# A postponed first transpose, a reordered normalisation and block transposes over every fourth key, in an attention kernel on one core

## The chip, the core and the metric

The kernel runs on one core of a Trainium2 chip. The time is that of the device for the whole program, in microseconds (us), as the median of several executions. The core has a matrix engine (TensorE, PE in the profile; its weight loads are PEld), a vector engine (VectorE, DVE), an activation engine (ScalarE, ACT), a general engine (GpSimd, POOL) and a queue for transfers (SyncE, SP). Each runs its own list of instructions in order and waits for the others on semaphores.

## The reference

The input x has 8 sequences of 1024 tokens with 256 channels. Attention with 16 heads of 64, then a residual sum and a layer norm; behind it a mixture of eight experts with a second residual sum and layer norm. The change touches only attention:

```python
latent_kv = x @ w_kv_down                # rank 128
k, v = split(latent_kv @ w_kv_up)        # 16 heads of 64
q = x @ w_q
att = einsum('bqhd,bkhd->bhqk', q, k) * 64 ** -0.5
att = softmax(where(causal, att, -inf), axis=-1)
y = einsum('bhqk,bkhd->bqhd', att, v)
x = layernorm(x + y @ w_out)
```

## The kernel before

attention_stage handles two heads (a pair) at a time, 64 pairs in all (8 sequences of 8 pairs). For each pair n it goes through eight tiles q of 128 queries. A "slot" is one step (n, q); each engine has a function `slot(n, q)` that lists by hand what it issues there. Causality makes tile q see q + 1 tiles of keys, so the tiles grow from 128 to 1024 columns. Score s = 2q + h is that of tile q for head h.

For a score: TensorE computes it (line 330), VectorE adds the mask and takes the maximum (`maximum`, line 651), ScalarE computes the exponential into one of eight buffers `prob` and the row sum (`exp`, line 514), VectorE inverts the sum (`invert`, line 657), and GpSimd multiplies the row by it (`norm`, line 209). The probabilities must then be turned, so that keys lie along the partitions, before they are multiplied with v (`pv`, line 376). There are two ways:

- tiles 0 to 3: TensorE transposes them (`turn`, line 358), ScalarE copies them out of PSUM into `tri` (`copy_turned`, line 532), one copy is VectorE's (line 672).
- tiles 4 to 7: VectorE transposes blocks of 32 by 32 (`turn_squares`, line 665) into `squares`. Four such blocks side by side are the keys of one tile of keys. SP writes `squares` to DRAM (`write_squares`, line 262) and reads it back with four transfers of 32 partitions each (`read_squares`, line 272) into `late_t`. In the kernel before, block j holds keys 32j to 32j + 31 and lands in partitions 32j to 32j + 31.

The same slots also hold the projections of q, k and v (lines 413 to 415, 426 to 428, 441) for the next pair, which are computed in a single PSUM bank, so that each waits for ScalarE's copy of the one before (`keep`, line 520, and `copy_v`, line 525). They use the weights split in a high part (ScalarE, line 546) and a low part (`weights_low`, GpSimd, line 215).

The counters set the order. `norm_done` counts normalised scores, so whoever waits for one must know its place in GpSimd's list. `exp` of scores 0 to 7 of a pair reuses buffers that hold scores 8 to 15 of the pair before, and waits until VectorE has turned them (`squared`). Scores share three areas of PSUM: those of tile 4 wait for the exponentials of tiles 2 and 3 (`scores_free`).

Behind the last pair, TensorE waits for the last reads of `late_t`, and then the output stage and the expert stage follow.

Of the kernel before, what the change touches and what calls it, by code (L numbers as in the profile page):

```python
# [17 lines left out]
P = 128  # L18
# [4 lines left out]
NPAIR = NH // 2  # L23
# [41 lines left out]
def attention_stage(nc, x_t, w_down, w_q, w_k, w_v, y_d, s_d, w_out, R):  # L65
# [4 lines left out]
    with ExitStack() as ctx:  # L70
# [95 lines left out]
        def y_place(n, g):  # L166
            return min(2 * n + 3, 2 * NPAIRS) if g else max(2 * n, 1)

        def last_of_batch(n):
            return n % NPAIR == NPAIR - 1 and n < NPAIRS - 1  # L170

# [18 lines left out]
        @block.gpsimd  # L190
        def _(pool):
            for free in (*pv_done, y_copied, *y_out):
                pool.sem_inc(free, 1)
            pool.memset(ident[:], 0.0).then_inc(const_ready, 1)
            pool.wait_ge(const_ready, 1)
            pool.affine_select(out=ident[:], in_=ident[:], compare_op=ALU.not_equal, fill=1.0, base=0,
                               pattern=[[-1, P]], channel_multiplier=1).then_inc(const_ready, 1)
            pool.wait_ge(const_ready, 2)
            pool.memset(mask[:], 0.0).then_inc(const_ready, 1)
            pool.wait_ge(const_ready, 3)  # L200
            pool.affine_select(out=mask[:, T - P:T], in_=mask[:, T - P:T], compare_op=ALU.is_ge, fill=-MASKED, base=0,
                               pattern=[[-1, P]], channel_multiplier=1).then_inc(const_ready, 1)

            def norm(n, q):
                pool.wait_ge(inv_done, 8 * n + q + 1)
                pool.sem_inc(passed, 1)
                for i in (2 * q % PB, 2 * q % PB + 1):
                    pr = prob[i][:, 0:(q + 1) * P]
                    pool.tensor_scalar(pr, pr, inv[:, i:i + 1], 1.0, ALU.mult, ALU.mult).then_inc(norm_done, 1)  # L209

            def weights_low(n):
                u = n % 2
                pool.wait_ge(w_high, n + 1)
                pool.sem_inc(passed, 1)
                pool.tensor_tensor(wqk_lo[u][:], wqk[u][:], wqk_hi[u][:].bitcast(F32), ALU.subtract).then_inc(w_low, 1)

            def x_low_part(b, i):
                k, cols = x_piece(i)
                pool.wait_ge(x_high, 4 * b + i + 1)
                pool.sem_inc(passed, 1)  # L220
                pool.tensor_tensor(xt_lo[:, k, cols], xt[:, k, cols], xt_hi[:, k, cols].bitcast(F32), ALU.subtract
                                   ).then_inc(x_low, 1)

            def l_low_part(b, i):
                pool.wait_ge(l_step, 4 * b + 2 * i + 2)
                pool.sem_inc(passed, 1)
                pool.tensor_tensor(lat_lo[:, halves(i)], lat[:, halves(i)], lat_hi[:, halves(i)].bitcast(F32),
                                   ALU.subtract).then_inc(l_low, 1)

            weights_low(0)  # L230

            def slot(n, q):
                norm(n, q)
                for i in x_pieces(n, q):
                    x_low_part(n // NPAIR + 1, i)
                if q == 0 and n + 1 < NPAIRS:
                    weights_low(n + 1)
                if last_of_batch(n) and q in (2, 3):
                    l_low_part(n // NPAIR + 1, q - 2)

            over_pairs(slot)

        @block.sync
        def _(sp):
# [19 lines left out]
            def read_squares(n, q):  # L264
                t = q + 1
                sp.wait_ge(squares_out[q % 2], 16 * (2 * n + (q - 4) // 2 + 1))
                sp.sem_inc(passed, 1)
                if q == 4 and n >= 2:
                    sp.wait_ge(pv_done[1], n)
                    sp.sem_inc(passed, 1)  # L270
                for j in range(4):
                    sp.dma_start(late_t[n % 2][Q * j:Q * j + Q, q - 4, :, 0:2 * t * Q],
                                 s_d[q - 4, :, 2 * j * t * Q:2 * (j + 1) * t * Q].rearrange("(i p) c -> p i c", p=Q)
                                 ).then_inc(late_in[n % 2], 16)

# [46 lines left out]
        def _(pe):  # L322
# [26 lines left out]
            def turn(n, q):  # L349
                if q:  # L350
                    pe.wait_ge(copied, 4 * n + q)
                elif n:
                    pe.wait_ge(exp_done, 16 * n)
                for h in range(2):
                    pe.wait_ge(norm_done, 16 * n + 2 * q + h + 1)
                    for j in range(q + 1):
                        to = q - j if h else j
                        mm = pe.transpose(turned_part(n, q, h)[:, to * P:(to + 1) * P],  # L358
                                          prob[(2 * q + h) % PB][:, j * P:(j + 1) * P], ident[:])
                    mm.then_inc(turned, 1)  # L360
# [92 lines left out]
            def slot(n, q):  # L453
# [9 lines left out]
                if q == 1:  # L463
                    if n >= 2:
                        pv(n - 2, 1, [6, 7])
                    project_v(n, 0)
                    turn(n, 0)
                if q == 2:
                    project_v(n, 1)
                    turn(n, 1)  # L470
                if q == 3:
                    if last_of_batch(n):
                        project_l(n // NPAIR + 1, 0)
                        turn(n, 2)
                        project_q(n + 1, 0)
                    else:
                        if after:
                            project_q(n + 1, 0)
                        turn(n, 2)
                if q == 4:  # L480
                    if last_of_batch(n):
                        project_l(n // NPAIR + 1, 1)
                        turn(n, 3)
                        project_k(n + 1, 0)
                    else:
                        if after:
                            project_k(n + 1, 0)
                        turn(n, 3)
                    if after:
                        project_k(n + 1, 1)  # L490
                if q == 5:
                    if after:
                        project_q(n + 1, 1)
                    pv(n, 0, range(4))
                if q == 6 and n:
                    pv(n - 1, 1, [0, 1, 2])
# [8 lines left out]
        def _(act):  # L505
# [74 lines left out]
            def slot(n, q):  # L580
# [15 lines left out]
                if q == 2:  # L596
                    if n >= 2:
                        copy_y(n - 2, 1)
                    copy_turned(n, 0)
                    exp(n, 4)  # L600
                    copy_v(n, 1)
                    exp(n, 5)
                if q == 3:
                    copy_turned(n, 1)
                    exp(n, 6)
                    if new:
                        l_split(n // NPAIR + 1, 0)
                    exp(n, 7)
                if q == 4:
                    if new:  # L610
                        copy_turned(n, 2)
                    if after:
                        keep(n + 1, 0)
                    if new:
                        l_split(n // NPAIR + 1, 1)
                    else:
                        copy_turned(n, 2)
                        if after:
                            keep(n + 1, 1)
                    exp(n, 8)  # L620
                    copy_turned(n, 3, [0])
                    if new:
                        keep(n + 1, 1)
                    exp(n, 9)
                if q == 5:
                    if after:
                        keep(n + 1, 2)
                    exp(n, 10)
                    if after:
                        keep(n + 1, 3)  # L630
                    exp(n, 11)
                if q == 6:
                    copy_y(n, 0)
# [11 lines left out]
        def _(dve):  # L645
# [10 lines left out]
                dve.wait_ge(exp_done, 16 * n + 2 * q + 2)  # L656
                dve.reciprocal(inv[:, i:i + 2], total[:, i:i + 2]).then_inc(inv_done, 1)  # L657

            def turn_squares(n, q):
                t = q + 1  # L660
                for h in range(2):
                    dve.wait_ge(norm_done, 16 * n + 2 * q + h + 1)
                    if h == 0:
                        dve.wait_ge(squares_out[q % 2], 16 * (2 * n + (q - 4) // 2))
                    dve.transpose(square_all(q).rearrange("p (j h k c) -> p j h k c", j=4, h=2, c=Q)[:, :, h, :, :],  # L665
                                  prob[(2 * q + h) % PB][:, 0:t * P].rearrange("p (k j c) -> p j k c", j=4, c=Q)
                                  ).then_inc(squared, 1)

            def copy_turned_last(n):
# [20 lines left out]
                                  ALU.subtract).then_inc(l_low, 1)  # L690

            def slot(n, q):
                maximum(n, 2 * q)
                if q == 3:
                    invert(n, 2)
                if q == 5:
                    invert(n, 4)
                maximum(n, 2 * q + 1)
                if q == 0 and n:
                    turn_squares(n - 1, 6)  # L700
                if q == 1:
                    if n:
                        invert(n - 1, 7)
                    invert(n, 0)
                if q == 2:
                    invert(n, 1)
                    if n:
# [2 lines left out]
                    invert(n, 3)  # L710
                if q == 4:
                    copy_turned_last(n)
                if q == 6:
                    invert(n, 5)
                    turn_squares(n, 4)
                if q == 7:
                    invert(n, 6)
                    turn_squares(n, 5)
                if n == NPAIRS - 1 and q < 4:
                    wo_low(q)  # L720

# [1288 lines left out]
```

## Time and profile before

| | us |
|---|---|
| median of 3 runs | 3476.64 |
| lowest and highest run | 3470.68, 3477.32 |
| the profiled execution | 3472.87 |
| its span of instructions | 3471.0 |
| TensorE busy in the span | 2987.7 |
| VectorE, ScalarE, GpSimd busy | 1971.3, 1776.9, 1568.1 |

The profile is one execution. Its page gives the busy time of each engine and cuts the span into 40 equal slices of 86.8 us; the attention stage fills slices 1 to 28. Groups name the line, the engine and what is written and read. A timeline lists instructions of one engine in order, those of one line and form merged; the number in brackets is how long the engine was idle before and who released it.

### The profile page before, as it was taken

How to read it: one execution, taken by the hardware profiler on the slowest of the kernel's cores; microseconds unless marked ns; L12 is line 12 of the kernel's file. 1: busy time of each engine (PE TensorE's matmuls, PEld its weight loads, DVE VectorE, ACT ScalarE, POOL GpSimd, SP SyncE). 2: the span in 40 equal slices, each digit the busy share in tenths (PEclk: the TensorE clock that was granted, in tenths of full speed). 3: DMA queues.
4: the chain of work that ended last, by engine and by line, in shares of the span. 5: the costliest groups of instructions: out<-in, count | busy, mean ns of one | idle time of the engine just before them, and what ended most of it. 6: DMA issues, size and time to landing. Idle time of an engine off the chain costs nothing. (4 is left out here: it accounts for less than half of the span.)

```text
span 3471.0 us, 53404 instructions
## 1 busy us (share of the span) xinstructions
PE 2987.7 (86%) x17196; PEld 1986.9 (57%) x17196; DVE 1971.3 (57%) x4808; ACT 1776.9 (51%) x3981; POOL 1568.1 (45%) x1661
## 2 busy tenths in 40 slices
PE   7788888887888887888888888885998999999997
PEld 4444444443444444444444444443998999999997
DVE  4555555555555555555555555554397885455446
ACT  5555555555555555555555555553544444444443
POOL 2334334333333433433343333331676777666665
PEclk9899899899898999899999998997999999999998
DMA  4886886887778777877877868878774444444335
GB/s 119 215 226 187 220 225 189 221 215 207 207 205 223 204 202 223 214 196 210 230 187 214 229 184 225 217 193 242 268 258 139 119 100 106 104 106 101 78 73 150
DMA packets 345525, 644.62 MB, mean 186 GB/s; under 512 B 36360, under 2 KB 244616, under 8 KB 337056
## 3 DMA queue, kind: packets, MB, share of 16 engines
q1 hardware_dynamic: 303200, 590.68, 61.4%
q0 software_dynamic: 25152, 33.75, 5.8%
q10 hardware_dynamic: 16896, 16.78, 1.4%
q8 instruction: 139, 2.28, 0.3%
q14 instruction: 138, 1.13, 0.1%
HBM read 347.38 MB, written 293.69 MB: 185 GB/s over the span
## 5 line engine op out<-in xcount | busy, mean ns | idle before, releaser
L209 POOL TENSOR_SCALAR prob<-prob,inv 128x128 f32<-128x128 f32 (+7 forms) x1024 | 748.9, 745 | 1485.0 <-DVE inv L657 1485.0
L651 DVE CUSTOM_DVE_ANT_0 s_ps<-s_ps,mask 128x128 f32<-128x128 f32 (+7 forms) x1024 | 756.6, 771 | 985.1 <-PE s_ps L330 985.1
L514 ACT ACTIVATE prob<-s_ps,neg_max 128x128 f32<-128x128 f32 (+7 forms) x1024 | 755.3, 739 | 820.3 <-DVE neg_max L651 820.3
L358 PE MATMUL s_ps<-ident,prob 128*128 128x128 f32 x1280 | 237.8, 313 | 357.6 <-POOL prob L209 357.6
L665 DVE STREAM_TRANSPOSE squares<-prob 128x640 f32<-128x640 f32 (+3 forms) x512 | 500.1, 1015 | 2.1 <-DMA s_d<-squares 2.1
L376 PE MATMUL o_ps<-late_t,v 128*64 128x512 f32 (+3 forms) x2048 | 414.5, 526 | 46.2 <-DMA late_t<-s_d 45.5
L358 PEld LDWEIGHTS s_ps<-ident,prob 128*128 128x128 f32 x1280 | 155.6, 152 | 445.9 <-issue 408.8
L330 PE MATMUL s_ps<-tok 64*128 64x512 f32 (+3 forms) x1536 | 344.9, 556 | 10.3 <-ACT tri L532 7.3
L330 PE MATMUL s_ps<-k,q 64*128 64x512 f32 (+3 forms) x1536 | 344.1, 554 | 10.6 <-ACT tri L532 7.8
L1670 PE MATMUL e_y<-w_hi,hid_hi 128*128 128x256 f32 (+1 forms) x1088 | 312.1, 287 | 0.0
L1672 PE MATMUL e_y<-w_hi,hid_lo 128*128 128x256 f32 (+1 forms) x1088 | 308.2, 283 | 0.0
L1671 PE MATMUL e_y<-w_lo,hid_hi 128*128 128x256 f32 (+1 forms) x1088 | 308.2, 283 | 0.0
L1531 POOL DMA_INDIRECT acc_d<-yg,idx_all x128 | 211.0, 1648 | 189.8 <-ACT yg L1744 155.8
L376 PEld LDWEIGHTS o_ps<-late_t,v 128*64 128x64 f32 x2048 | 124.9, 136 | 281.8 <-issue 187.1
L1778 ACT ACTIVATE raw<-e_h,b1s 128x384 f32<-128x384 f32 (+3 forms) x336 | 193.8, 586 | 133.9 <-PE e_h L1653 128.2
L330 PEld LDWEIGHTS s_ps<-tok 64*128 64x128 f32 x1536 | 135.7, 199 | 181.3 <-issue 128.1
L330 PEld LDWEIGHTS s_ps<-k,q 64*128 64x128 f32 x1536 | 134.8, 198 | 180.4 <-issue 120.3
L1651 PE MATMUL e_h<-tok_hi,w_hi 128*128 128x384 f32 (+3 forms) x672 | 229.9, 342 | 1.7 <-DVE tok_lo L1816 1.2
L1652 PE MATMUL e_h<-tok_lo,w_hi 128*128 128x384 f32 (+3 forms) x672 | 229.8, 342 | 0.0
L1653 PE MATMUL e_h<-tok_hi,w_lo 128*128 128x384 f32 (+3 forms) x672 | 229.4, 341 | 0.0
L532 ACT ACTIVATE tri<-s_ps 128x128 f32<-128x128 f32 (+3 forms) x448 | 164.4, 412 | 119.3 <-PE s_ps L358 114.0
L441 PEld LDWEIGHTS j_ps<-wv,b_lat 128*128 128x128 f32 x1024 | 173.9, 257 | 80.0 <-issue 79.4
(233 smaller groups left out, 5545.1 us busy)
## 6 DMA issues: line engine op xcount, KB each, us to landing
s_d<-squares SPq DMA_DIRECT2D x64, 1024.0 KB, 5.1
late_t<-s_d SPq DMA_DIRECT2D x256, 256.0 KB, 6.9
s_d<-squares SPq DMA_DIRECT2D x64, 896.0 KB, 7.0
late_t<-s_d SPq DMA_DIRECT2D x256, 224.0 KB, 6.6
s_d<-squares SPq DMA_DIRECT2D x64, 768.0 KB, 4.0
late_t<-s_d SPq DMA_DIRECT2D x256, 192.0 KB, 6.9
s_d<-squares SPq DMA_DIRECT2D x64, 640.0 KB, 2.9
late_t<-s_d SPq DMA_DIRECT2D x256, 160.0 KB, 5.1
```

Source lines behind the costliest of these rows:

```text
L209: pool.tensor_scalar(pr, pr, inv[:, i:i + 1], 1.0, ALU.mult, ALU.mult).then_inc(norm_done, 1)
L330: mm = pe.matmul(score_part(n, 2 * q + h)[:, w], q_of[n % 2][rows, cols], k_of[n % 2][rows, w], start=True, stop=True)
L358: mm = pe.transpose(turned_part(n, q, h)[:, to * P:(to + 1) * P], prob[(2 * q + h) % PB][:, j * P:(j + 1) * P], ident[:])
L376: mm = pe.matmul(o_ps[64 * h:64 * h + 64, off:HALF], v[n % 2][:, k, 64 * h:64 * h + 64], keys, start=(k == 0), stop=(k == 4 * g + 3), skip ...
L514: act.activation(prob[i][:, 0:(q + 1) * P], score_part(n, s), ACT.Exp, scale=-1.0, bias=neg_max[:, i:i + 1], accum_out=total[:, i:i + 1]). ...
L651: dve.tensor_tensor_reduce(part, part, mask[:, T - (q + 1) * P:T], 1.0, -MASKED, ALU.add, ALU.min, neg_max[:, i:i + 1]).then_inc(max_done, 1)
L665: dve.transpose(square_all(q).rearrange("p (j h k c) -> p j h k c", j=4, h=2, c=Q)[:, :, h, :, :], prob[(2 * q + h) % PB][:, 0:t * P].rear ...
L1651: pe.matmul(out, w1_hi[u][:, w], tok_hi[:, k, 0:N], start=(k == 0), stop=False)
L1652: pe.matmul(out, w1_hi[u][:, w], tok_lo[:, k, 0:N], start=False, stop=False)
L1670: pe.matmul(out, hid_hi[:, m, cols], w2_hi[u][:, w], start=(m == 0), stop=False)
L1671: pe.matmul(out, hid_hi[:, m, cols], w2_lo[u][:, w], start=False, stop=False)
L1672: mm = pe.matmul(out, hid_lo[:, m, cols], w2_hi[u][:, w], start=False, stop=(m == HC - 1))
```

## The change

TensorE issues its transposes of tiles 0, 1 and 2 one slot later, those of tile 3 stay in slot 4; the last projection of q moves from slot 5 to slot 4, ahead of the scores of tile 5. ScalarE's copies follow. GpSimd normalises tile 7 of a pair behind tile 0 of the next, and splits the next weights one slot later, behind tile 1. VectorE turns tile 4 in slot 5 rather than 6, tile 5 at the head of slot 7, and tile 6 in slot 1 of the next pair, one head ahead of the inverse of tile 0 and one behind it. The block transposes read every fourth column of a tile, so that block j holds keys j, j + 4, j + 8 and so on, and the read back into `late_t` puts it into partitions j, j + 4, j + 8. What `late_t` holds in the end is the same.

```diff
+        def normal(n, q, h):
+            place = {0: max(8 * n - 1, 0), 7: min(8 * n + 8, 8 * NPAIRS - 1)}.get(q, 8 * n + q)
+            return 2 * place + h + 1
@@ GpSimd
             def slot(n, q):
-                norm(n, q)
+                if q < 7:
+                    norm(n, q)
+                if q == 0 and n:
+                    norm(n - 1, 7)
+                if q == 1 and n + 1 < NPAIRS:
+                    weights_low(n + 1)
                 for i in x_pieces(n, q):
                     x_low_part(n // NPAIR + 1, i)
-                if q == 0 and n + 1 < NPAIRS:
-                    weights_low(n + 1)
@@ SP
-                    sp.dma_start(late_t[n % 2][Q * j:Q * j + Q, q - 4, :, 0:2 * t * Q],
+                    sp.dma_start(late_t[n % 2][j:P:4, q - 4, :, 0:2 * t * Q],
@@ TensorE
                 if q == 1:
...
                     project_v(n, 0)
-                    turn(n, 0)
                 if q == 2:
                     project_v(n, 1)
-                    turn(n, 1)
+                    turn(n, 0)
                 if q == 3:
...
                         if after:
                             project_q(n + 1, 0)
-                        turn(n, 2)
+                        turn(n, 1)
                 if q == 4:
...
                         if after:
                             project_k(n + 1, 0)
-                        turn(n, 3)
+                        turn(n, 2)
                     if after:
                         project_k(n + 1, 1)
-                if q == 5:
+                    turn(n, 3)
                     if after:
                         project_q(n + 1, 1)
+                if q == 5:
                     pv(n, 0, range(4))
@@ ScalarE
                 if q == 2:
                     if n >= 2:
                         copy_y(n - 2, 1)
-                    copy_turned(n, 0)
                     exp(n, 4)
                     copy_v(n, 1)
                     exp(n, 5)
                 if q == 3:
-                    copy_turned(n, 1)
+                    copy_turned(n, 0)
                     exp(n, 6)
...
                     exp(n, 7)
                 if q == 4:
...
                     else:
-                        copy_turned(n, 2)
+                        copy_turned(n, 1)
                         if after:
                             keep(n + 1, 1)
+                        copy_turned(n, 2)
+                    if after:
+                        keep(n + 1, 2)
                     exp(n, 8)
                     copy_turned(n, 3, [0])
...
                     exp(n, 9)
                 if q == 5:
                     if after:
-                        keep(n + 1, 2)
+                        keep(n + 1, 3)
                     exp(n, 10)
-                    if after:
-                        keep(n + 1, 3)
                     exp(n, 11)
@@ VectorE
                     dve.transpose(square_all(q).rearrange("p (j h k c) -> p j h k c", j=4, h=2, c=Q)[:, :, h, :, :],
-                                  prob[(2 * q + h) % PB][:, 0:t * P].rearrange("p (k j c) -> p j k c", j=4, c=Q)
+                                  prob[(2 * q + h) % PB][:, 0:t * P].rearrange("p (k c j) -> p j k c", j=4, c=Q)
...
             def slot(n, q):
-                maximum(n, 2 * q)
                 if q == 3:
                     invert(n, 2)
-                if q == 5:
-                    invert(n, 4)
+                if q == 7:
+                    turn_squares(n, 5)
+                maximum(n, 2 * q)
+                if q > 4:
+                    invert(n, q - 1)
                 maximum(n, 2 * q + 1)
-                if q == 0 and n:
-                    turn_squares(n - 1, 6)
                 if q == 1:
                     if n:
                         invert(n - 1, 7)
+                        turn_squares(n - 1, 6, [0])
                     invert(n, 0)
+                    if n:
+                        turn_squares(n - 1, 6, [1])
                 if q == 2:
                     invert(n, 1)
                     if n:
...
                 if q == 4:
                     copy_turned_last(n)
-                if q == 6:
-                    invert(n, 5)
+                if q == 5:
                     turn_squares(n, 4)
-                if q == 7:
-                    invert(n, 6)
-                    turn_squares(n, 5)
```

## Rows read from the trace of the kernel before

**Rows 1.** The page: TensorE's busy share, and in tenths over 40 slices.

```profile
PE 2987.7 (86%) x17196; PEld 1986.9 (57%) x17196; DVE 1971.3 (57%) x4808; ACT 1776.9 (51%) x3981; POOL 1568.1 (45%) x1661
...
PE   7788888887888887888888888885998999999997
```

**Rows 2.** Waits within 100 to 2300 us: total, times, longest.

```profile
PE s_ps L358 <- POOL prob L209: 331.8, 178, 6.2
...
PEld o_ps L376 <- DMA late_t<-s_d: 45.1, 50, 1.9
```

**Rows 3.** TensorE's timeline of pairs in mid-stage: start, us, instruction [idle before].

```profile
1513.26 1.56 PE L330 MATMUL s_ps<-k,q 64*128 64x512 f32 x8 [0.25 <-ACT tri L532]
...
1529.52 1.16 PE L441 MATMUL j_ps<-wv,b_lat 128*128 128x128 f32 x8
1535.62 0.73 PE L358 MATMUL s_ps<-ident,prob 128*128 128x128 f32 x2 [4.93 <-POOL prob L209]
1536.27 1.65 PE L330 MATMUL s_ps<-tok 64*128 64x384 f32 x4
1537.86 1.82 PE L441 MATMUL j_ps<-wv,b_lat 128*128 128x128 f32 x8
```

**Rows 4.** TensorE's timeline of pair 0: scores 0, scores 2, v projection 1.

```profile
17.53 0.49 PE L330 MATMUL s_ps<-k,q 64*128 64x128 f32 x4
...
21.35 0.92 PE L330 MATMUL s_ps<-k,q 64*128 64x384 f32 x4
22.20 1.16 PE L441 MATMUL j_ps<-wv,b_lat 128*128 128x128 f32 x8
```

**Rows 5.** Timelines of ScalarE (exp 10) and VectorE in the same pairs.

```profile
1516.06 0.90 ACT L514 ACTIVATE prob<-s_ps,neg_max 128x768 f32<-128x768 f32 x1 [1.59 <-DVE neg_max L651]
...
1527.67 1.82 DVE L665 STREAM_TRANSPOSE squares<-prob 128x768 f32<-128x768 f32 x2
...
1529.83 2.10 DVE L665 STREAM_TRANSPOSE squares<-prob 128x896 f32<-128x896 f32 x2
...
1532.55 0.22 DVE L657 RECIPROCAL inv<-total 128x2 f32<-128x2 f32 x2
```

**Rows 6.** GpSimd's timeline at the seam of two pairs.

```profile
1532.91 2.90 POOL L209 TENSOR_SCALAR prob<-prob,inv 128x1024 f32<-128x1024 f32 x4 [2.96 <-DVE inv L657]
1535.78 0.99 POOL L215 TENSOR_TENSOR w_lo<-wqk,w_hi 128x384 fp32r<-128x384 f32 x1
1539.48 0.93 POOL L209 TENSOR_SCALAR prob<-prob,inv 128x256 f32<-128x256 f32 x2 [2.71 <-DVE inv L657]
```

**Rows 7.** Busy us of PE, PEld, DVE, ACT, POOL in windows; then clock, DMA share, GB/s.

```profile
1535.62:1537.86 2.24, 2.24 (x7) 0.79 (x7) 0.00 (x0) 0.45 (x2) 1.16 (x2) 0.55 1.02 364
...
1499.57:1535.62 36.05, 30.39 (x151) 15.52 (x151) 20.50 (x49) 19.57 (x48) 12.65 (x18) 0.92 0.80 212
```

**Rows 8.** VectorE's groups by form: count, busy us, mean ns of one.

```profile
L665 DVE STREAM_TRANSPOSE squares<-prob 128x1024 f32<-128x1024 f32 x128 | 150.4, 1213 | 2.1 <-DMA s_d<-squares 2.1
...
L665 DVE STREAM_TRANSPOSE squares<-prob 128x640 f32<-128x640 f32 x128 | 99.2, 813 | 0.0
...
L1822 DVE TENSOR_TENSOR hid_lo<-raw,hid_hi 128x512 fp32r<-128x512 f32 x112 | 75.6, 685 | 0.0
...
L1912 DVE CAST hid_hi<-raw 128x512 fp32r<-128x512 f32 x112 | 48.3, 431 | 64.1 <-ACT raw L1778 64.1
```

**Rows 9.** Transfers: a write alone (1524.5 to 1527.5), reads (1548 to 1552), SP's wait.

```profile
q1 hardware_dynamic: 144, 0.66, 54.0%
...
DMA packets 514, 0.87 MB, mean 218 GB/s; under 512 B 58, under 2 KB 298, under 8 KB 514
...
SPq L285 <- DMA late_t<-s_d: 12.5, 2, 6.3
```

**Rows 10.** TensorE's timeline at the last pair: first scores, and behind the last wait.

```profile
2337.60 0.49 PE L330 MATMUL s_ps<-tok 64*128 64x128 f32 x4
...
2403.04 7.39 PE L376 MATMUL o_ps<-late_t,v 128*64 128x512 f32 x32 [26.45 <-DMA late_t<-s_d]
```

More of the change, by code:

```diff
@@ L232, in slot @@
             def slot(n, q):
-                norm(n, q)
+                if q < 7:
[4 more added lines that the diff above has]
+                    weights_low(n + 1)
                 for i in x_pieces(n, q):
                     x_low_part(n // NPAIR + 1, i)
-                if q == 0 and n + 1 < NPAIRS:
-                    weights_low(n + 1)
-                if last_of_batch(n) and q in (2, 3):
-                    l_low_part(n // NPAIR + 1, q - 2)
+                if last_of_batch(n) and q == 2:
+                    for i in range(2):
+                        l_low_part(n // NPAIR + 1, i)
             over_pairs(slot)
+            norm(NPAIRS - 1, 7)
         @block.sync
@@ L354, in turn @@
                 for h in range(2):
-                    pe.wait_ge(norm_done, 16 * n + 2 * q + h + 1)
+                    pe.wait_ge(norm_done, normal(n, q, h))
                     for j in range(q + 1):
@@ L478, in slot @@
                             project_q(n + 1, 0)
-                        turn(n, 2)
+                        turn(n, 1)
                 if q == 4:
@@ L487, in slot @@
                             project_k(n + 1, 0)
-                        turn(n, 3)
+                        turn(n, 2)
                     if after:
                         project_k(n + 1, 1)
-                if q == 5:
+                    turn(n, 3)
                     if after:
                         project_q(n + 1, 1)
+                if q == 5:
                     pv(n, 0, range(4))
@@ L615, in slot @@
                         l_split(n // NPAIR + 1, 1)
+                        copy_turned(n, 2)
+                        keep(n + 1, 1)
                     else:
-                        copy_turned(n, 2)
+                        copy_turned(n, 1)
                         if after:
                             keep(n + 1, 1)
+                        copy_turned(n, 2)
+                    if after:
+                        keep(n + 1, 2)
                     exp(n, 8)
                     copy_turned(n, 3, [0])
-                    if new:
-                        keep(n + 1, 1)
                     exp(n, 9)
@@ L657, in invert, with turn_squares @@
                 dve.reciprocal(inv[:, i:i + 2], total[:, i:i + 2]).then_inc(inv_done, 1)
-            def turn_squares(n, q):
+            def turn_squares(n, q, heads=range(2)):
                 t = q + 1
-                for h in range(2):
-                    dve.wait_ge(norm_done, 16 * n + 2 * q + h + 1)
+                for h in heads:
+                    dve.wait_ge(norm_done, normal(n, q, h))
                     if h == 0:
```

## The prediction

> **What bounds the kernel now.** First I read the page [rows 1]: TensorE is busy 86% of the span, but only 7 to 8 tenths in the first 27 slices of 40, which are the attention stage, and 9 tenths behind it. The change touches the attention stage alone. Its last head pair issues its first scores at 2337.60 [rows 10] and its first pair at 17.53 [rows 4], so 63 steps take 2320.1 us, 36.8 each. Second, the waits inside that stage [rows 2]: the only large wait of TensorE is that of the transposes (line 358) for GpSimd's normalisation, 331.8 us in 178 waits; for the transfers of late_t it waits 45.1, never over 1.9 at a time. The other engines aren't full: in a period of 36.05 us VectorE is busy 20.5, ScalarE 19.57, GpSimd 12.65 and the DMA engines 80% [rows 7]. Third, one pair on TensorE [rows 3]: a period, from the first transposes at 1499.57 to the next at 1535.62, holds one long hole of 4.93 us, ahead of the transposes of tile 0. Why it is there shows on the other engines [rows 5, 6]: VectorE puts the block transposes of tiles 5 and 6 of the pair before (1527.67 to 1531.9) ahead of the maxima of tile 1, and inverts tile 0's sum only at 1532.55; GpSimd then first scales tile 7 of the pair before, and tile 0 at last.
>
> The hole costs twice. In the 2.24 us behind it the granted clock is 0.55 of full, so nearly all of them at 1.2 GHz rather than 2.4, after 4.93 us in which TensorE did nothing [rows 3, 7]. Scores of tile 2 take 1.65 us and the second v projection 1.82 [rows 3]; in pair 0, which has no long hole, they take 0.92 and 1.16 [rows 4]. With 0.3 for the first transposes this is (0.73 + 0.66 + 0.3) = 1.7 us a pair. TensorE's busy time in a period is 30.39 [rows 7], so its work at full clock is 28.7 us.
>
> **The change part by part.** I lay out one pair [rows 3 to 6], t = 0 at the issue of the scores of tile 0, from which the first v projection's end (1530.68) is 4.66 us off; of operations that repeat in each pair, the rows show one or two.
>
> *First transposes one slot later.* Transposes of tiles 0, 1 and 2 go behind the scores of the next tile, and on GpSimd tile 0 is scaled ahead of tile 7. Tile 0's inverse comes at about t = 5.6, its scaling (2 x 0.36) ends at 6.7, and TensorE asks for it at 7.6, behind scores 2 and v projection 1. The hole of 4.93 and the 1.7 of clock go. What comes late next:
>
> *(a) v projection 1 behind ScalarE.* It needs the copy of v projection 0, which stands behind exp 0 to 3 and the weights' copy. ScalarE ends exp 15 at t = 3.5; five short operations of 0.36 to 0.6 more put the copy's end at 6.3, while scores 2 end at 5.5. Gap 0.9.
>
> *(b) The q projection behind GpSimd.* weights_low is moved behind norm(n,7) and norm(n,1). GpSimd: tile 0 to 6.7, tile 7 (2 x 1.1) to 8.9, tile 1 (0.93) to 9.8, weights_low (0.99) to 10.8 [rows 6]. Scores 3 end at 9.2, and project_q stands right behind them, ahead of the transposes of tile 1, so nothing covers the rest. Gap 1.7. In the kernel before weights_low was done at 1536.77, while the scores of tile 2 ran, and its use came behind those of tile 3.
>
> *(c) Scores 4 behind VectorE.* They need exp 7, exp 7 needs maximum 7, and the block transposes of tile 7 stand ahead of maximum 6. They end at t = 9.7 at today's price, which hides fully; each 0.1 us more on a block transpose of tile 6 or 7 delays exp 7 by 0.1, four times over.
>
> *The block transposes themselves.* Their count and shapes stay (8 a pair, 640 to 1024 columns), but each reads every fourth column, 16 bytes apart. No row shows such a read on VectorE. The lower end is today's price, 813 to 1213 ns, or 1.04 ns a column and 0.15 fixed [rows 8]; a gain is excluded, since no column is saved. For the upper end I take the widest ratio between two rates at one shape in this trace: a cast of 512 columns 431 ns and a two-operand operation of 512 columns 685 [rows 8], less 0.15 fixed nearly 1 to 2. So up to 2.08 ns a column, twice as many column times. Neither row is nearer, so I take the middle, 1.56 ns: 1.15, 1.35, 1.56 and 1.75 us. With it the transposes of tile 7 end at 11.8, exp 7 at 14.0, scores 4 could go at 13.25: gap 0.9. The transposes of tiles 4 and 5 end 0.3 and 0.6 later than the scores of tiles 6 and 7 would let the maxima start; 0.15 of it reaches TensorE. The total for VectorE is 20.5 + 3.5 = 24.0 us a pair, so it is not full.
>
> The Trainium skill, "Vector Engine (DVE) Microarchitecture Reference", the table under the SBUF access granule, states 1.73 ns a column where one source hops at every element, against 1.054 in runs. By that price the gaps are 0.6 us a pair larger and the sum would be about 3295. No run here shows it yet.
>
> *Copies reordered, q projection 1 ahead of scores 5.* Transposes 3 follow k projection 1 at once and wait for the copy of tile 2 behind two keeps: gap 0.35. Scores 5 then have 1.6 us more cover for exp 8 and the last copies: no wait. But exp 10, due before scores 6, loses that cover: exp 10 ends 3.7 us after scores 5 begin (1513.26 to 1516.96) [rows 3, 5], while scores 5 and pv take 3.8. Zero, with nothing to spare.
>
> *Transfers to partitions four apart.* The bytes and pieces stay. The reads of late_t now run at 218 GB/s while the DMA engines are all busy; a write of squares moves 0.66 MB in 54% of 3 us, 405 GB/s [rows 9]. So the reads, 3.4 MB a pair, take 15.6 us and may take between that and 8.4. In the steady pairs this is hidden: SP's queue waits up to 6.3 us for the last read [rows 9], but TensorE hardly [rows 2]. From the end of tile 7's block transposes to the first use of late_t the new order leaves 15.3 us (t = 11.8 to 27.1), about what the order before leaves. That is enough even at 218, with 28.8 of 32.7 us of DMA time used, though barely. If it isn't, the wait lands in the pv of slot 6. Only behind the last pair it is open: TensorE waits 26.45 us [rows 10]; reads 6 and 7 (1.97 MB) need 9.0 at 218 and 4.9 at 405. The skill's "SBUF — State Buffer", on the DMA port swizzle, says that 32 neighbouring partitions reach 8 of 16 ports, and every fourth one, by its formula, reaches all. I take 4 us gained from the rows, less 1 for the slower transposes: 3 (bounds -1 and 8).
>
> **Sum.** Period 28.7 + 0.9 + 1.7 + 0.9 + 0.15 + 0.35 = 32.7 us, 3.35 less than 36.05. Times 63 is 211; with 3 of the tail 214. The profiled execution took 3472.87 (its span 3471.0), 3.8 under the median of the runs. 3472.87 - 214 = 3259, rounded to 3260.
>
> **The rivals.** (1) *The spread read costs nothing.* Then gap (c) and the 0.15 go, (a) shrinks to 0.4 and (b) to 1.5: period 31.0, 5.05 x 63 = 318, plus tail, about 3150. For it: the trace's transposes run at one column a cycle whatever their order of blocks. Against: all of them read runs of 32. (2) *The spread read costs twice a column or more, slower than before.* Place: VectorE's queue between maximum 5 and maximum 6. At 2.08 ns the block transposes of tiles 6 and 7 end at 14.2, exp 7 at 16.4, scores 4 wait 2.6, (a) is 1.6, (b) 1.8, slot 6 and 7 lose 0.8 and tile 3 0.35: period 35.9, 3460. With holes of that size the low clock is back, 1.7 more: 37.6, 1.55 x 63 = 98, about 3570. It decides from 2 times the column price upwards; between, 3500. [...] (3) *The transfers don't gain, or lose.* If the reads stay at 218 the sum moves by 4; if partitions four apart made them slower than 218, the load of 28.8 of DMA time a pair [rows 7] would bound the period at 33 or more: 3280 to 3400. (4) *The hole only moves*, because the clock drops at the sum of small gaps: 1.7 of 3.35 is lost, about 3365.
>
> **How the numbers follow.** Forecast (1.3 to 1.7 times a column's time) 0.44, rival 1 0.26, rival 2 0.19, rival 3 0.06, rival 4 0.05. The range reaches from the better side of rival 1 to the better end of rival 2: 3120 to 3450, which leaves out some 0.2. The forecast's own range is 3220 to 3340. A measurement of this kernel tells apart about 0.2%, 7 us. Rival 2 gives 0.04 to faster, 0.02 to the same and 0.13 to slower; rival 3 0.05 to faster and 0.01 to slower; the others are all faster. Faster 0.84, same 0.02, slower 0.14.
>
> **What would show it.** In the changed kernel: the line of the block transposes by shape (1.15 to 1.75 us; 0.8 to 1.2 for rival 1; 1.5 to 2.3 and more for rival 2). The 4.93 us wait of line 358 gone, and scores 2 at 0.92 rather than 1.65. A wait of the q projection (line 413) for weights_low (line 215) of over 1 us a pair; if GpSimd is earlier, (b) is wrong. Waits of scores for ScalarE's exp at tile 4. Rate of a late_t read above 218 GB/s. The prediction is wrong if VectorE's queue is full or the granted clock stays at 0.92.

## The result and the profile after

The changed kernel takes 3290.01 us (median of 3 runs, 3277.38 to 3291.08) against 3476.64: a ratio of 0.946, 95% interval 0.942 to 0.950. The forecast was 3260 with a range of 3120 to 3450. The profiled execution took 3290.01, 182.9 less than that of before (3472.87).

The page of the changed kernel (lines of the helpers moved: scores are L340, transposes L368, block transposes L675, the reads' users L386, the q projection L423, weights_low L220):

```profile
PE 2916.1 (89%) x17196; PEld 1973.4 (60%) x17196; DVE 2307.4 (70%) x4808; ACT 1753.8 (53%) x3981; POOL 1568.3 (48%) x1661
...
PE   7898888888888898888888888869999999999997
```

TensorE's total shrank by 72 us with the same number of instructions, which is clock, and VectorE's grew by 336 [rows 1]. Waits of the changed kernel within 100 to 2150 us, to be read beside rows 2, and two of its whole span:

```profile
PEld j_ps L423 <- POOL w_lo L220: 175.3, 53, 3.5
...
PE j_ps L423 <- POOL w_lo L220: 131.4, 53, 2.7
PE s_ps L340 <- ACT prob L524: 91.0, 162, 1.8
...
PE j_ps L423 <- ACT b_lat L570: 20.9, 7, 3.0
...
PE o_ps L386 <- DMA late_t<-s_d: 20.8, 1, 20.8
```

The wait for GpSimd's normalisation, 331.8 us before [rows 2], is off the list. In its place stand the wait for weights_low and the one for exponentials. One pair on TensorE (timeline, idle before in brackets), beside rows 3:

```profile
1512.48 0.49 PE L340 MATMUL s_ps<-k,q 64*128 64x128 f32 x4
...
1515.13 0.70 PE L340 MATMUL s_ps<-k,q 64*128 64x256 f32 x4 [0.51 <-ACT prob L524]
...
1517.66 0.92 PE L340 MATMUL s_ps<-k,q 64*128 64x384 f32 x4
1518.77 1.16 PE L451 MATMUL j_ps<-wv,b_lat 128*128 128x128 f32 x8 [0.19 <-ACT v L535]
1519.76 0.38 PE L368 MATMUL s_ps<-ident,prob 128*128 128x128 f32 x2
1520.07 1.13 PE L340 MATMUL s_ps<-k,q 64*128 64x512 f32 x4
1523.69 0.80 PE L423 MATMUL j_ps<-b_xt_hi,w_hi 128*128 128x512 f32 x1 [2.48 <-POOL w_lo L220]
1524.28 0.63 PE L424 MATMUL j_ps<-b_xt_lo,w_hi 128*128 128x512 f32 x1
...
1527.60 1.35 PE L340 MATMUL s_ps<-k,q 64*128 64x512 f32 x8 [0.53 <-ACT prob L524]
...
1545.47 0.49 PE L340 MATMUL s_ps<-tok 64*128 64x128 f32 x4
```

From scores 0 to the next scores 0 it is 32.99 us, where it was 36.05 [rows 7]. Scores 2 take 0.92 us rather than 1.65 and v projection 1 takes 1.16 rather than 1.82 [rows 3]: the clock is full there. The largest hole is now 2.48 us ahead of the q projection, and the low clock follows that one: its matmuls take 0.63 rather than 0.40. The windows of this pair (busy PE, PEld, DVE, ACT, POOL, then clock, DMA share, GB/s), beside rows 7:

```profile
1512.48:1545.47 32.99, 28.85 (x152) 15.21 (x151) 25.76 (x50) 19.14 (x48) 12.64 (x17) 0.95 0.77 264
...
1523.69:1527.60 3.91, 3.38 (x10) 2.48 (x11) 3.04 (x7) 1.59 (x5) 1.15 (x2) 0.64 0.95 322
```

VectorE in the same pair, and two of its groups by form beside rows 8 (mean ns last ahead of the bar):

```profile
1516.80 1.81 DVE L675 STREAM_TRANSPOSE squares<-prob 128x896 f32<-128x896 f32 x1
...
1518.56 1.86 DVE L675 STREAM_TRANSPOSE squares<-prob 128x896 f32<-128x896 f32 x1
...
1521.33 3.94 DVE L675 STREAM_TRANSPOSE squares<-prob 128x1024 f32<-128x1024 f32 x2
...
1525.21 0.70 DVE L661 CUSTOM_DVE_ANT_0 s_ps<-s_ps,mask 128x512 f32<-128x512 f32 x1
```

```profile
L675 DVE STREAM_TRANSPOSE squares<-prob 128x1024 f32<-128x1024 f32 x128 | 251.4, 2010 | 1.4 <-POOL prob L214 1.4
...
L675 DVE STREAM_TRANSPOSE squares<-prob 128x640 f32<-128x640 f32 x128 | 165.8, 1335 | 8.4 <-POOL prob L214 0.8
```

VectorE goes from the block transposes of tile 6 over the maxima of tile 2 to those of tile 7 without a pause, and maximum 6 starts when they end, 12.7 us into the pair. The price went from 813 and 1213 ns [rows 8] to 1335 and 2010, that is (2010 - 1335) / 384 = 1.76 ns a column.

### The profile page after: what moved, and what is told of

Read it like the earlier page. It is cut to its first block and busy times, and to the rows that moved or that the text cites. A ratio compares the mean times of both kernels' runs of the same rounds, so it can differ in the third digit from the quotient of the medians.

```text
span 3288.2 us, 53404 instructions
## 1 busy us (share of the span) xinstructions
PE 2916.1 (89%) x17196; PEld 1973.4 (60%) x17196; DVE 2307.4 (70%) x4808; ACT 1753.8 (53%) x3981; POOL 1568.3 (48%) x1661
## 5 line engine op out<-in xcount | busy, mean ns | idle before, releaser
L214 POOL TENSOR_SCALAR prob<-prob,inv 128x256 f32<-128x256 f32 (+7 forms) x1024 | 748.6, 747 | 1286.4 <-DVE inv L667 1286.4
L675 DVE STREAM_TRANSPOSE squares<-prob 128x640 f32<-128x640 f32 (+3 forms) x512 | 840.8, 1679 | 15.4 <-POOL prob L214 2.2
L386 PE MATMUL o_ps<-late_t,v 128*64 128x512 f32 (+3 forms) x2048 | 415.7, 528 | 22.7 <-DMA late_t<-s_d 20.8
L340 PE MATMUL s_ps<-tok 64*128 64x512 f32 (+3 forms) x1536 | 335.3, 542 | 55.0 <-ACT prob L524 54.1
L340 PE MATMUL s_ps<-k,q 64*128 64x512 f32 (+3 forms) x1536 | 328.3, 532 | 51.3 <-ACT prob L524 50.7
L386 PEld LDWEIGHTS o_ps<-late_t,v 128*64 128x64 f32 x2048 | 126.2, 136 | 256.0 <-issue 216.0
L340 PEld LDWEIGHTS s_ps<-tok 64*128 64x128 f32 x1536 | 137.7, 197 | 236.5 <-issue 187.4
L340 PEld LDWEIGHTS s_ps<-k,q 64*128 64x128 f32 x1536 | 134.6, 192 | 226.6 <-issue 177.0
L423 PE MATMUL j_ps<-b_xt_hi,w_hi 128*128 128x512 f32 x252 | 125.5, 498 | 156.5 <-POOL w_lo L220 135.6
L1921 DVE CAST hid_hi<-raw 128x384 fp32r<-128x384 f32 (+3 forms) x336 | 128.6, 383 | 122.6 <-ACT raw L1787 116.5
L368 PE MATMUL s_ps<-ident,prob 128*128 128x128 f32 x1280 | 207.3, 296 | 5.0 <-ACT tri L542 4.3
L524 ACT ACTIVATION_READ_ACCUMULATOR prob<-s_ps,neg_max 128x1 f32 x1024 | 205.0, 200 | 0.0
```

Source lines behind the costliest of these rows:

```text
L340: mm = pe.matmul(score_part(n, 2 * q + h)[:, w], q_of[n % 2][rows, cols], k_of[n % 2][rows, w], start=True, stop=True)
L386: mm = pe.matmul(o_ps[64 * h:64 * h + 64, off:HALF], v[n % 2][:, k, 64 * h:64 * h + 64], keys, start=(k == 0), stop=(k == 4 * g + 3), skip ...
L524: act.activation(prob[i][:, 0:(q + 1) * P], score_part(n, s), ACT.Exp, scale=-1.0, bias=neg_max[:, i:i + 1], accum_out=total[:, i:i + 1]). ...
```

## The experiments

All times are medians of four runs, with the kernel before run beside them on the same chip (3471.75 us for the order alone, the run with permuted rows, the whole layout and weights_low earlier; 3476.81 for the partitions alone, every second partition and the two with keys reordered in the scores; 3472.38 for the rest). A gain in us is against that one. A difference between medians of two groups can be off by some 5 us for that reason; where it matters, both figures are given. Theory A at the start: the block transposes on VectorE set the period of the changed kernel; the transfers are hidden.

**The order alone.** Block transposes and partitions as in the kernel before.

```diff
-  late_t[n % 2][j:P:4, ...]         ...rearrange("p (k c j) -> p j k c", ...)
+  late_t[n % 2][Q * j:Q * j + Q, ...]  ...rearrange("p (k j c) -> p j k c", ...)
```

> The changed kernel's order, but block transposes over runs of 32 columns and transfers into 32 neighbouring partitions, as in the kernel before. Theory A: block transposes back to 0.81 to 1.21 us, the period is 31.0 us as worked out for the free spread read, 2 less than 33.0: about 3160 us (3140 to 3180), with the wait for weights_low at about 1.5 us. Rival C (the transfers need the spread partitions): reads at 218 GB/s take 15.6 us of a period, DMA engines over 90% busy, TensorE waits for late_t, 3200 us or more.

Measured 3304.36 us (ratio 0.952, 0.950 to 0.954). Theory A's 3160 fell, and with it the sentence that the transfers are hidden. TensorE's and SP's waits of this kernel (100 to 2000 us):

```profile
PE o_ps L386 <- DMA late_t<-s_d: 143.5, 50, 4.5
...
SPq L277 <- DMA s_d<-squares: 373.5, 159, 5.8
```

and its transfers from 1500 to 1566, and of 3 us with reads alone:

```profile
q1 hardware_dynamic: 7782, 16.33, 91.7%
...
DMA packets 396, 0.64 MB, mean 214 GB/s; under 512 B 43, under 2 KB 359, under 8 KB 396
```

In these 66 us the queue's packets take 91.7% of the DMA engines' time; over 100 to 2000 us the DMA share is 0.85. Writes of 1024 KB now land after 8.1 us in the median (5.4 in the changed kernel), and SP waits 373.5 us for writes before it may issue the reads (52.8 in the changed kernel). TensorE finds late_t missing in 50 pairs. The wait costs twice here too: in 24 of these pairs the matmuls of `pv` behind the wait take 4.1 to 5.4 us rather than 2.8.

**Runs of 32, reads still into every fourth partition.** This is called the run with permuted rows below. It differs from the last in the partitions alone, and from the changed kernel in the columns alone.

```diff
-  ...rearrange("p (k c j) -> p j k c", j=4, c=Q)
+  ...rearrange("p (k j c) -> p j k c", j=4, c=Q)
```

> As the order alone (runs of 32 columns), but the reads still land in every fourth partition. It leaves out that the keys of tiles 4 to 7 stand where v has them: those rows of late_t are permuted. Theory A: same period as the order alone, within 0.2 us, so a difference under 15 us, all of it in the wait behind the last pair (some 4 us) and in hidden transfers; reads at 350 GB/s rather than 218. Rival C: clearly faster than the order alone, by 30 us or more.

Measured 3096.27 us (0.892, 0.890 to 0.893), 208 under the order alone: rival C holds in the new order. Its period is 31.0 us, as worked out for a free spread read. Its DMA share from 100 to 2000 us is 0.73, writes of 1024 KB land after 5.9 us, SP waits 79.3 us for writes, and TensorE's matmuls wait for late_t 0.2 us in all. Against the changed kernel it is 194 us less (189 with each against its own run of the kernel before), the price of the spread columns: 3.0 to 3.1 us a pair on average.

**The partitions alone, in the kernel before.**

> The kernel before, order and block transposes unchanged, with only the reads landing in every fourth partition. It leaves out that the keys of tiles 4 to 7 stand where v has them. Theory D (the transfers bound only the new order: at 36 us a pair the engines need 80% and keep up, at 31 they would need over 90% and don't): less than 10 us faster than the kernel before, from the wait behind the last pair; the transfers' share falls from 0.80 to about 0.65. Rival E (the transfers cost the kernel before as much as they cost the order alone, 208 us): 3270 us.

Measured 3447.56 us (0.992, 0.990 to 0.993), 29 less, not under 10. Theory D's mechanism holds (29 is far from 208), but its size was short. TensorE's waits for late_t in the whole span, here and in the kernel before:

```profile
PE o_ps L376 <- DMA late_t<-s_d: 22.8, 1, 22.8
```

```profile
PE o_ps L376 <- DMA late_t<-s_d: 45.5, 31, 26.4
```

Thirty short waits and 3.6 us of the last one are gone, 22.7 us together. So the transfers were already a small limit before; the other 6 us of the 29 are not traced.

**The whole layout alone, in the kernel before.** Spread columns and partitions, old order.

> The kernel before with the layout alone: block transposes over every fourth column, reads into every fourth partition; the order of work stays. Block transposes of tiles 5 and 6 stand ahead of tile 0's inverse, which sets the hole of 4.93 us; they cost 2 x 0.62 and 2 x 0.72 more. Theory A: the hole grows by 2.7 us, and tile 7's 1.6 more ahead of maximum 6 shows in part: 2.7 to 4.3 us a pair, 3640 to 3750 us. Rival C: the faster reads win it back in part, under 3600.

Measured 3650.43 us (1.051, 1.049 to 1.053). The hole ahead of the first transposes grew as laid out, from 4.93 [rows 3] by 2.56:

```profile
1530.46 0.73 PE L358 MATMUL s_ps<-ident,prob 128*128 128x128 f32 x2 [7.49 <-POOL prob L209]
```

Between the medians this is 203 us for the columns over the partitions alone (208 with each against its own run of the kernel before), near the 194 (189) they cost in the new order. The layout without the order is a loss of 179 us.

**Which partitions.** Runs of 32 and the new order, reads into every second partition of one half.

```diff
-  late_t[n % 2][j:P:4, ...]
+  late_t[n % 2][64 * (j // 2) + j % 2:64 * (j // 2) + 64:2, ...]
```

> As the run with permuted rows (runs of 32, new order), but a read lands in every second partition of one half of 64, not in every fourth of 128. It leaves out that the keys of tiles 4 to 7 stand where v has them. Theory H (what counts is how many of the 16 write paths a single transfer reaches; 32 partitions of one half reach 8, as the neighbouring ones do): reads at about 218 GB/s and 3300 us, as the order alone. Rival I (any distance between partitions helps): about 3096 to 3200 us.

Measured 3275.78 us (0.942, 0.940 to 0.943): close to the order alone, far from 3096, so theory H holds but for 29 to 34 us, which no run explains. Four us of it that are nearly all reads; below it the changed kernel in 1 us of reads alone (1531 to 1532) and in 4 us with a write and reads:

```profile
DMA packets 526, 0.87 MB, mean 218 GB/s; under 512 B 59, under 2 KB 397, under 8 KB 526
```

```profile
DMA packets 222, 0.35 MB, mean 350 GB/s; under 512 B 27, under 2 KB 222, under 8 KB 222
...
DMA packets 640, 1.58 MB, mean 396 GB/s; under 512 B 68, under 2 KB 416, under 8 KB 544
```

The table of ports in the Trainium skill ("SBUF — State Buffer", Door 1: The DMA port swizzle) gives 32 neighbouring partitions and every second one of a half 8 of 16 ports, and every fourth partition all 16. The rates agree: 214 and 218 GB/s for the first two sets, 350 for the third.

**Which columns.** As the changed kernel, but each block reads every second column, 8 bytes apart (the blocks start 16 columns apart and so overlap).

> The changed kernel, but the block transposes read every second column (8 bytes apart) instead of every fourth (16 bytes). It leaves out that all columns of a tile are turned and stand where v has them. Measured so far: 1.04 ns a column in runs of 32, 1.76 with steps of four. Theory J (a read that lands in a new 16-byte line each time costs; two reads in one line do not): 0.81 to 1.2 us for a block transpose and about 3096 us. Rival K (any element that has no neighbour next to it costs the same): 1.34 to 2.01 us and 3290 us.

Measured 3095.15 us (0.892, 0.890 to 0.893). The block transposes by form:

```profile
L677 DVE STREAM_TRANSPOSE squares<-prob 128x1024 f32<-128x1024 f32 x128 | 151.9, 1225 | 2.3 <-POOL prob L214 1.4
...
L677 DVE STREAM_TRANSPOSE squares<-prob 128x640 f32<-128x640 f32 x128 | 103.8, 846 | 8.5 <-POOL prob L214 0.8
```

In the run with permuted rows, which reads runs of 32 in the same order, they take 1224 and 845 ns. Theory J holds: steps of 8 bytes cost nothing, steps of 16 cost 0.7 to 0.8 ns a column.

**weights_low earlier.** In the changed kernel the largest hole waits for it. First it is put ahead of tile 7's normalisation:

```diff
-                if q == 0 and n:
-                    norm(n - 1, 7)
-                if q == 1 and n + 1 < NPAIRS:
+                if q == 0 and n + 1 < NPAIRS:
                     weights_low(n + 1)
+                if q == 0 and n:
+                    norm(n - 1, 7)
```

> The changed kernel, with weights_low put back between the normalisations of tile 0 and tile 7. In the changed kernel TensorE waits 2.5 us a pair for it (line 423 for line 220), then 0.5 for the exponentials ahead of scores 4. Theory A (VectorE's block transposes set the period): the wait for weights_low goes, but scores 4 still wait for exp 7 at the same place, so the period of 33.0 us stays, or falls by up to 0.7 where the clock no longer drops behind the hole: 3245 to 3290 us. Rival B (weights_low sets the period): the period falls by about 2 us, 63 times: about 3165 us.

Measured 3380.81 us (0.974, 0.972 to 0.976): slower than the changed kernel by 91 to 96, which neither theory said. Part could be tile 7's delay, so a second kernel delays nothing: the weights are split a pair earlier in idle time, weights_high in slot 7 ahead of exp 14 and weights_low ahead of the normalisation of tile 6.

> The changed kernel with its spread read, and the weights split a pair earlier in idle time of ScalarE and GpSimd. The wait for weights_low (2.5 us a pair) goes and nothing else is delayed. Theory A (VectorE's chain sets exp 7 and with it scores 4): the wait reappears ahead of scores 4, 3.5 us in one piece, the period doesn't fall; the low clock behind it costs 1 to 1.6 us on work that nothing hides: 3290 to 3390 us. Rival B (weights_low sets the period): 3140 us.

Measured 3351.26 us (0.965, 0.964 to 0.967), still 61 to 66 slower, and inside theory A's range. TensorE's timeline of the first (two rows), then of the second:

```profile
1521.73 1.95 PE L340 MATMUL s_ps<-k,q 64*128 64x512 f32 x8 [3.64 <-ACT prob L524]
...
1529.60 1.56 PE L340 MATMUL s_ps<-k,q 64*128 64x512 f32 x8
```

```profile
1534.69 2.50 PE L342 MATMUL s_ps<-tok 64*128 64x512 f32 x8 [3.29 <-ACT prob L526]
```

The wait is back ahead of scores 4, in one piece of 3.3 to 3.6 us, because exp 7 comes when VectorE is through. Scores 4 take 1.95 and 2.50 us rather than 1.35. In the first, from scores 4 to scores 5 it is 7.87 us; in the changed kernel it is 6.30 (1527.60 to 1533.90). The granted clock there is 0.78 against 1.00. That is 1.6 us of low clock in this pair on work that nothing hides; scores 4 also come 0.3 us later (15.4 rather than 15.1 behind scores 0), and the rest of the pair is alike. Over the 55 steps inside a sequence the mean is 35.1 us, in the changed kernel 33.5, which makes 89 us; the steps over a border of sequences are alike. In the changed kernel the low clock falls mostly on the q projection, which ends before exp 7 does. So the wait for weights_low hides under VectorE's chain (theory A), and rival B fell twice.

**The keys' order made elsewhere.** The spread partitions want keys in steps of four, but the block transposes need not make them. First TensorE reads k in steps of four for the scores of tiles 4 to 7, with the mask's triangle to match:

```diff
+                        if q >= 4:
+                            keys = keys.rearrange("r (k c j) -> r k j c", j=4, c=Q)
```

> The changed kernel, but the keys' order is made elsewhere: TensorE reads every fourth key when it computes the scores of tiles 4 to 7, so that block transposes read runs of 32 again and still land in every fourth partition; the mask's last 128 columns follow. The output is complete. Theory A (the spread read on VectorE costs 3 us a pair and nothing else stands in its way): 3096 us, as the run with permuted rows. Rival F (TensorE pays for the spread read instead, 24 of its matmuls a pair): up to 0.5 us each, 3300 us and more.

Measured 3444.3 us (0.991, 0.989 to 0.993): rival F. The same group in the run with permuted rows and here:

```profile
L340 PE MATMUL s_ps<-tok 64*128 64x512 f32 x734 | 206.1, 653 | 3.2 <-ACT prob L524 2.4 <-issue 0.8
```

```profile
L346 PE MATMUL s_ps<-tok 64*128 64x512 f32 x624 | 290.6, 1030 | 0.0
```

This mean still holds the scores of tile 3, 4 of 24 in a pair, which read neighbours. Scores 7 alone (1505.89), eight matmuls of 64x512, have a mean of 1091 ns where the run with permuted rows has 616 (1503.79), and take 3.85 us together rather than 1.99:

```profile
1505.89 3.85 PE L346 MATMUL s_ps<-k,q 64*128 64x512 f32 x8
```

With weights_low early as well:

> As the kernel with the keys reordered in the scores, and weights_low put ahead of the normalisation of tile 7. Theory A: with the short block transposes VectorE no longer holds scores 4 back at once, so now the wait for weights_low (1.96 us a pair) is in part real: about 1 us a pair gained, 3030 us (3000 to 3060). Rival G (as in the run with the spread read: the hole moves ahead of scores 4, and the low clock lands on work that nothing hides): 3100 us or more.

Measured 3518.16 us (1.012, 1.010 to 1.013): rival G again, 74 us slower than without.

Then ScalarE makes the order when it copies k, and keeps a plain copy of the first half for tiles 0 to 3:

```diff
+                if i == 1:
+                    out = k_first[:]
+                if i == 2:
+                    out, made = in_blocks(out, made)
...
+            def first_keys_in_blocks(n):
+                act.wait_ge(high_done, 4 * n + 2)
+                out, keys = in_blocks(k_of[n % 2][:, halves(0)], k_first[:])
+                act.activation(out, keys, ACT.Copy).then_inc(in_order, 1)
```

> The changed kernel, with the keys' order made when ScalarE copies k out of PSUM: k of tiles 4 to 7 stands in blocks, k for tiles 0 to 3 in its own buffer, one copy of 512 columns a pair more on ScalarE, in slot 6; the mask is bf16 to make room. VectorE's block transposes read runs of 32, the reads land in every fourth partition, and TensorE reads k in runs. The output is complete. Theory A: 3096 us as the run with permuted rows, plus up to 20 us for the two copies with a spread read on ScalarE: 3096 to 3130. Rival L (ScalarE's spread read of PSUM delays exp 8 and scores 5): over 3150.

Measured 3098.15 us (0.892, 0.891 to 0.894): theory A, and a complete kernel 192 us faster than the changed one (188 with each against its own run of the kernel before). Its copies by form:

```profile
L551 ACT ACTIVATE tok<-k_first 128x512 f32<-128x512 f32 x32 | 36.3, 1136 | 0.0
...
L542 ACT ACTIVATE k<-j_ps 128x512 f32<-128x512 f32 x31 | 18.5, 598 | 13.2 <-PE j_ps L443 13.2
```

The spread copy out of SBUF takes 1136 ns, where ScalarE's conversion of 512 neighbouring columns from SBUF (b_xt) takes 623 in the same run. The spread copy out of PSUM takes 598, as a plain one does (k_first, 598). Both fit into ScalarE's idle time. On this kernel, the weights a pair earlier:

> As the kernel whose keys ScalarE reorders, and the weights are split a pair earlier, where ScalarE (slot 7) and GpSimd (ahead of the normalisation of tile 6) are idle; nothing is put ahead of tile 7. Theory M (with short block transposes the wait for weights_low, 2 us a pair, is what holds the pair): about 1 us a pair less than the kernel without it, 60 us. Rival G (the wait turns up ahead of scores 4 in one piece and the low clock lands on what follows): no gain or slower.

Measured 3037.91 us (0.875, 0.873 to 0.876), 60 less as theory M said, and the fastest here: 12.5% under the kernel before, 7.7% under the changed one (3037.91 / 3290.01, from different groups of runs). What is left of the hole, 1.76 us, waits for exp 7:

```profile
1535.01 1.35 PE L347 MATMUL s_ps<-k,q 64*128 64x512 f32 x8 [1.76 <-ACT prob L533]
```

## Why the prediction was right, and where not

*The hole and its clock.* Right: 4.93 us gone, scores 2 at 0.92.

*The period.* 32.7 forecast, 32.99 measured. Idle in it was 4.0 forecast and is 4.14 (32.99 - 28.85), but distributed otherwise, by the letters of the prediction. (a) 0.9 forecast; it is 0.19, and 0.51 came ahead of scores 1, where exp 14 is late because block transposes of tile 5 hold maximum 14 back. (b) 1.7 forecast, 2.48 measured: TensorE reached the q projection at t = 8.7, not 9.2, and weights_low ended 0.3 later. (c) 0.9 forecast, 0.53 measured, but only because 1.3 us of low clock in the q projection filled the rest (3.38 us busy behind the hole, where the same work takes 2.06 at full clock in the kernel with weights_low ahead of tile 7). The gap of 0.35 ahead of transposes 3 isn't there, and the 0.15 for tiles 6 and 7 is 0.29 ahead of scores 7. Errors of both signs cancelled; that the total is better than its parts is luck.

*The price of the spread read.* The mis-sized term: 1.56 ns a column taken from the middle of two rows, 1.76 measured, or 1.34 to 2.01 us a transpose where 1.15 to 1.75 stood. The source was far off (a cast against a two-operand operation). The Trainium skill's table ("Vector Engine (DVE) Microarchitecture Reference", the SBUF access granule) says 1.73 ns for one source that hops 4 KiB at every element. The steps here are 16 bytes, and the 1.76 agrees in size; the sum by that price, 3295, is nearer to 3290 than mine, though with the same cancelling errors in its other terms. The same passage of the Trainium skill asks for runs of two adjacent words for the full rate; the run with every second column has none adjacent and loses nothing, so here the measurement decides. The Trainium skill's "SBUF — State Buffer" (Door 1, the note on cachelines), which asks for at least two hits on a 16-byte line, fits both measurements.

*The 63 steps.* 3.06 us in a plain pair would be 193. From pair 0 to pair 63 the scores 0 moved from 2320.1 us apart [rows 4, 10] to 2142.2 (16.50 to 2158.74), 178. Of the 15 us that are missing, some 6 are at the borders of sequences, whose seven steps went from 41.5 to 39.3 us on average: there are seven new waits of 3.0 us for l_split (20.9 us above), since the latent's copy stands behind exp 6, and that behind VectorE. Two are in the first step. The other 7 or so are in the 55 steps inside a sequence, on average 36.4 before and 33.5 now: 16 of them take 33.9 to 35.3 rather than 33.0. In one (from 1784.35, 34.6 us) the low clock began later and lay on scores 4:

```profile
1799.43 2.51 PE L340 MATMUL s_ps<-k,q 64*128 64x512 f32 x8 [0.60 <-ACT prob L524]
```

Scores 4 take 2.51 us there rather than 1.35, and nothing hides it. The forecast took one pair of before, 63 times.

*The tail.* 3 forecast, 5.6 measured (26.45 to 20.8).

*The transfers.* The step that failed: "That is enough even at 218", and rival 3's "the sum moves by 4". In the order alone the transfers cost 208 us, at a period that is 31.0 us without those waits. I added up the bytes against the period and counted the time from the last block transpose, but each read waits on SP for its own write to land, and under this load the writes land late (8.1 us, 5.9 with spread partitions). The waits on SP (373.5 us against 79.3) fit delays that add up along the one queue. The reads themselves also land later (256 KB after 6.5 us rather than 4.2), and no run separates the two. The forecast came out because the change holds the remedy. Had it been the order alone, 3160 would have missed by 144. Measured in parts, each against its own run of the kernel before: order -167, partitions -29 in the old order and -208 in the new, columns +208 and +189. The changed columns with neighbouring partitions were not run, so what the reads at 218 would cost at the changed kernel's period of 33 us stays open.

*Rival 2* (twice the price) would have decided at 2.08 ns; 1.76 is short of it. *Rival 4* was half right: the clock is 0.95 in the period, not full, but in most pairs its loss hides.

## What to carry to other kernels

When a change mends one resource (the partitions of a transfer) at the price of another (columns read on VectorE), look for a third place where the same order costs nothing; here two copies of the keys on ScalarE, which had idle time, were worth some 190 us. A wait that shows at the top of the list is worth what comes late next: ask for that before moving anything, and ask which work the low clock behind the hole will fall on. Transfers that make a chain (write, land, issue, read) on one queue can hold a kernel up below full use: here TensorE waited at a DMA share of 0.85.

## What the runs showed of the hardware

- Reads from DRAM of 32 partitions by one transfer ran at 214 to 218 GB/s into neighbouring partitions, and at 218 into every second one of a half; into every fourth of 128 they ran at 350 GB/s (1 us of reads alone), and the DMA engines moved 396 GB/s in 4 us of write and reads.
- Elements 16 bytes apart cost more in SBUF than neighbours, on three engines: VectorE's block transposes 1.76 rather than 1.04 ns a column, TensorE's moving operand 1091 rather than 616 ns for 64x512 (scores 7), ScalarE's copy of 512 columns 1136 ns where a conversion of 512 neighbouring columns takes 623. Elements 8 bytes apart cost VectorE's block transposes nothing (1225 and 1224 ns for 1024 columns), and elements 16 bytes apart in PSUM cost ScalarE nothing (598 and 598 ns).
- TensorE's clock was low behind single holes of 2.5 us and more, and full at two holes of 0.5 and 0.2 us in the same pair. It stayed full behind holes of 1.0 and 1.2 us (the two kernels with earlier weights on the changed one). Behind holes of 1.76 us (the fastest kernel) and 1.96 us (the one with permuted rows) it was full at first, and then 0.56 and 0.54 for a stretch.
